# Splitting seven experts' weights where they are used instead of staging them through DRAM, in a fused attention and mixture-of-experts kernel

## The chip, the cores and the metric

The kernel runs on one core of a Trainium2 chip. The metric is the time of one execution on the device, in microseconds; of several runs the median counts. The core has TensorE (matrix products), VectorE, ScalarE and GpSimd (elementwise work on 128 partitions), SyncE (here it only issues DMAs) and 16 DMA engines that all queues share. Each engine runs its own instruction stream in order, and the streams meet only in semaphores.

## What is computed

Four sequences of 512 tokens with 256 features attend to four contexts of 1024 tokens, and each token then goes through a shared expert and two of eight routed experts:

```python
x = x + tanh(g_xattn) * attention(layernorm(x), ctx, ctx, Wq, bq, Wk, bk, Wv, bv, Wo, bo)   # 16 heads of 16
z = layernorm(x)
shared = swiglu(z @ sw1 + sb1) @ sw2 + sb2
probs  = softmax(z @ gate_w + gate_b);  top 2 of 8 experts
routed = sum over the 2 experts of prob * (swiglu(z @ rw1[e] + rb1[e]) @ rw2[e] + rb2[e])
x = x + tanh(g_ffn) * (shared + routed)
```

All data are float32. Each of the nine experts (shared and eight routed) has 2*512 + 2*256 = 1536 weights on each of 128 partitions, 768 KB.

## The kernel before

Nearly every product is made as a sum of parts: a float32 operand is split into a high part (the value in TensorE's reduced float32 format) and a low part (the value minus the high part), and three products of parts are added. So each expert's weights must be cast and subtracted once before use. The result takes 24 units of 128 columns in the tile `wall`, 12 of the high part and 12 of the low part.

Phase A projects queries, keys and values for four batches (`b`). The attention loop follows: 16 units, four batches times four groups of four heads (`u`), and in each unit eight key blocks (`k`). TensorE makes the scores, ScalarE the exponentials, TensorE the sums of values, and beside that TensorE and VectorE find the row maxima for the next unit, which GpSimd splits in three parts (`split_max`).

During attention the local memory has no room for all experts. Two experts (EARLY) are split into their place by GpSimd in the first units (`prepare`). The seven others (LATE) have their places where attention keeps its operands. In the units 2 to 8 GpSimd's `stage(e)` splits one each in a buffer `wraw` and sends both parts to the DRAM tensor `w_parts`; `raw_in` loads the next. In the last batch places come free unit by unit, and SyncE's `late_weights(e, nth)` loads both parts of one expert, 1536 KB, each load after the one before it has landed: the first three during the units 1 to 3 of the last batch, the fourth when all scores are made, the fifth when all values are summed, the last two once batch 3's attention output has been turned.

The last batch is unrolled, with router work beside attention: for batch 0 to 2, TensorE turns the attention output (`r_attn`, L1564), multiplies by Wo (`r_wo`, L1571), VectorE adds it to x and takes the layer norm's statistics (`r_sum`, L1157 first) and scales (`r_scale`, with nine small operations in L1172 to L1174 and four scalings in L1176), TensorE turns and makes the logits, VectorE ranks the experts (`r_choose`) and makes the token slots (`r_slots`). The orders are written out by hand for every engine. `r_attn(b)` on TensorE waits for `wo_taken`, b times, that is for L1157 of the batch before.

After attention comes the hand-off: the same steps for batch 3, with the shared expert's first and second products (`first`, `second`) in between, ScalarE's `silu` and `gated_high`, VectorE's `gate`, `gated_low` and `base`. GpSimd scatters the normalised rows with indirect DMAs into `zs`, ordered by expert (`scatter`). Between `scatter(1)` and `scatter(2)` GpSimd blanks a tile `fill` and writes blank rows to `acc`, and SyncE writes blank rows and their ids to the spare rows of `zs`. Then 39 tiles of 128 routed tokens follow, each with the weights of its expert, whose place and number TensorE reads from a table made at run time; GpSimd adds each tile's result to `acc` with an indirect DMA, and at the end `acc` is copied to the output.

## Time and profile before

| | us |
|---|---|
| median of 3 timed runs | 705.16 |
| lowest and highest | 701.01, 708.19 |
| span of the profiled execution, first to last instruction | 716.3 |
| TensorE busy in it | 643.1 (90%) |
| VectorE busy | 482.2 (67%) |
| ScalarE busy | 424.1 (59%) |
| GpSimd busy | 229.7 (32%) |

The profiled execution's own time beside its span isn't given; its span alone is 11.1 us above the timed median. Phase A takes the first 105 us or so, the attention loop lasts until about 514, the hand-off until 583.7, and the tiles until about 699. A busy share is an average over these stretches; what ends a wait must be read from each.

### The profile page before, as it was taken

How to read it: one execution, taken by the hardware profiler on the slowest of the kernel's cores; microseconds unless marked ns; L12 is line 12 of the kernel's file. 1: busy time of each engine (PE TensorE's matmuls, PEld its weight loads, DVE VectorE, ACT ScalarE, POOL GpSimd, SP SyncE). 2: the span in 40 equal slices, each digit the busy share in tenths (PEclk: the TensorE clock that was granted, in tenths of full speed). 3: DMA queues.
4: the chain of work that ended last, by engine and by line, in shares of the span. 5: the costliest groups of instructions: out<-in, count | busy, mean ns of one | idle time of the engine just before them, and what ended most of it. 6: DMA issues, size and time to landing. Idle time of an engine off the chain costs nothing.

```text
span 716.3 us, 12642 instructions
## 1 busy us (share of the span) xinstructions
PE 643.1 (90%) x3603; PEld 335.5 (47%) x3616; DVE 482.2 (67%) x805; ACT 424.1 (59%) x842; POOL 229.7 (32%) x240
## 2 busy tenths in 40 slices
PE   3997769699999999999999999999885989999990
PEld 3775542123233333333333333355363778888880
DVE  4786878668888888888888888838726843443330
ACT  4675344567777777777777777767513224544440
POOL 2343242213431443134000221020175414555552
PEclk9999997989999999999999999999986999999995
DMA  7999889754688678966664370250386355555545
GB/s 232 343 251 336 200 257 159 124 76 108 147 159 200 197 162 147 218 185 161 97 103 59 62 117 1 89 208 30 137 299 217 135 174 97 98 95 94 78 49 141
DMA packets 82978, 108.21 MB, mean 151 GB/s; under 512 B 16552, under 2 KB 64690, under 8 KB 81973
## 3 DMA queue, kind: packets, MB, share of 16 engines
q1 hardware_dynamic: 72200, 78.97, 47.7%
q0 software_dynamic: 10736, 28.71, 15.0%
q8 instruction: 22, 0.36, 0.2%
q14 instruction: 20, 0.16, 0.1%
HBM read 62.10 MB, written 47.35 MB: 153 GB/s over the span
## 4 chain that ended last, share of the span: by engine, by line
PE 71%; issue 14%; POOL 5%; DVE 3%; DMA 3%; another core or an unknown queue 1%; ACT 1%; POOLq 1%; SPq 0%; DVEq 0%; ACTq 0%
PE psO L1503 17%; PE psS L1476 16%; PE psM L1458 13%; PE psH L1721 7%; PE psY L1747 3%; PE psH L1677 3%; POOL parts L610 3%; PE psX L1571 1%; PE psX L1709 1%; PE psH L1732 1%; DMA acc<-ysb,ids 1%; DMA wA_raw<-wqkv 1%; PE psO L1546 1%; PE psX L1663 1%
## 5 line engine op out<-in xcount | busy, mean ns | idle before, releaser
L1109 DVE TENSOR_REDUCE mneg<-psM 128x1 f32<-128x1024 f32 x240 | 282.8, 1220 | 67.7 <-PE psM L1458 67.6
L843 ACT ACTIVATE pr<-psS 128x512 f32<-128x512 f32 x488 | 266.7, 595 | 102.1 <-PE psS L1476 102.1
L1476 PE MATMUL psS<-kq 99*128 99x512 bf16 x488 | 153.8, 388 | 7.0 <-DMA kq<-msb 6.3
L1503 PE MATMUL psO<-pr,vt 128*32 128x512 f32 x1024 | 137.2, 608 | 0.0
L1458 PE MATMUL psM<-kq 96*128 96x512 bf16 x480 | 128.2, 388 | 4.4 <-DVE mneg L1109 2.7
L1476 PEld LDWEIGHTS psS<-kq 99*128 99x128 bf16 x488 | 39.9, 97 | 155.4 <-ACT pr L843 130.3
L750 POOL DMA_INDIRECT acc<-ysb,ids x39 | 60.2, 1543 | 69.0 <-ACT ysb L966 37.3
L1458 PEld LDWEIGHTS psM<-kq 96*128 96x128 bf16 x480 | 46.7, 98 | 63.6 <-DVE mneg L1109 8.4
L596 POOL TENSOR_TENSOR msb<-mcp,none 16x128 bf16<-16x128 f32 x16 | 6.2, 389 | 209.1 <-ACT mcp L820 209.0
L1721 PE MATMUL psH<-wall,zgT 128*128 x234 | 68.2, 427 | 1.5 <-DVE zgT L1341 1.5
L1347 DVE TENSOR_TENSOR rg<-psH,rs 128x256 f32<-128x256 f32 x39 | 16.6, 425 | 66.3 <-ACT rs L954 64.6
L1721 PEld LDWEIGHTS psH<-wall,zgT 128*128 128x128 f32 x234 | 44.5, 190 | 8.2
L610 POOL TENSOR_TENSOR parts<-kf,parts 128x512 bf16<-128x512 f32 x24 | 30.5, 1285 | 55.0 <-ACT parts L791 55.0
L954 ACT ACTIVATE rs<-psH 128x256 f32<-128x256 f32 x39 | 14.9, 383 | 42.8 <-PE psH L1721 41.7
L705 POOL DMA_INDIRECT zs<-zx,slot_u x32 | 32.2, 1006 | 23.4 <-DVE slot_u L1228 13.5
L1747 PE MATMUL psY<-wall,gT 128*128 x234 | 37.0, 294 | 0.0
L1503 PEld LDWEIGHTS psO<-pr,vt 128*32 128x32 f32 x1024 | 20.2, 108 | 35.5 <-issue 33.8
L1677 PE MATMUL psH<-zT,wall 128*128 128x512 f32 x96 | 29.5, 452 | 5.6 <-issue 5.6
L1747 PEld LDWEIGHTS psY<-wall,gT 128*128 128x128 f32 x234 | 30.2, 189 | 0.5
L966 ACT ACTIVATE ysb<-psY,zg 128x256 f32<-128x256 f32 x39 | 18.6, 476 | 17.4 <-PE psY L1747 14.7
L1416 PE MATMUL psV<-wAH,tH 128*128 128x256 f32 x64 | 16.7, 347 | 12.2 <-DVE tL L1027 12.2
L1033 DVE TENSOR_REDUCE mneg<-psO 128x1 f32<-128x1024 f32 x16 | 19.6, 1223 | 9.3 <-PE psO L1400 9.1
(243 smaller groups left out, 821.1 us busy)
## 6 DMA issues: line engine op xcount, KB each, us to landing
kq<-k_parts SPq DMA_DIRECT2D x96, 128.0 KB, 5.7
w_parts<-wraw POOLq DMA_DIRECT2D x14, 768.0 KB, 4.3
wall<-w_parts SPq DMA_DIRECT2D x7, 1536.0 KB
v_pad<-vst SPq DMA_DIRECT2D x16, 512.0 KB, 8.7
vt<-v_pad SPq DMA_DIRECT2D x16, 512.0 KB, 7.6
wraw<-wexp POOLq DMA_DIRECT2D x9, 768.0 KB, 7.2
k_parts<-parts SPq DMA_DIRECT2D x16, 384.0 KB, 6.3
kq<-q_parts SPq DMA_DIRECT2D x96, 64.0 KB, 5.3
```

What stands on the lines that cost most here:

```text
L610: nc.gpsimd.tensor_tensor(parts[:, c, m, 2], kf[:, m], parts[:, c, m, 1], ALU.subtract).then_inc(k_ok, 1)
L705: nc.gpsimd.indirect_dma_start(out=zs[:, :], out_offset=bass.IndirectOffsetOnAxis(ap=slot_u[:, b, k * QT + t:k * QT + t + 1], axis=0), in_ ...
L750: nc.gpsimd.indirect_dma_start(out=acc[:, :], out_offset=bass.IndirectOffsetOnAxis(ap=ids[:, i:i + 1], axis=0), in_=ysb[:, i % YB], in_off ...
L843: nc.scalar.activation(pr[:, slot, j], score_bank(s, j), ACT.Exp, scale=SCALE).then_inc(e_done, 1)
L1033: V.tensor_reduce(mneg[:, 0, i:i + 1], psE, X_AXIS, ALU.max, negate=True).then_inc(m_free, 1)
L1109: V.tensor_reduce(mneg[:, parity, i:i + 1], psM[:, i % 2], X_AXIS, ALU.max, negate=True).then_inc(m_free, 1)
L1458: last = mm(psM[:, i % 2, half * BLK:(half + 1) * BLK], qst[0:SROWS, slot, h, qt * P:(qt + 1) * P], kst[0:SROWS, slot, h, half * BLK:(half ...
L1476: mm(score_bank(s, j), kst[:, slot, j, kt * P:(kt + 1) * P], qst[:, slot, j], start=True, stop=True).then_inc(s_full, 1)
L1503: last = mm(psO[j * VW:(j + 1) * VW, u % 2], vt[:, u, k, j * VW:(j + 1) * VW], pr[:, k % 4, j], start=(k == 0), stop=(k == KT - 1), skip_g ...
L1677: last = mm(psH[:, j, ab], w1(SH, wp)[:, 4 * k + m], zT(b)[:, zp, k], start=(i == 0 and k == 0), stop=(i == 2 and k == DT - 1))
L1721: last = mm(psR[:, i % 2], zgT[:, i % 2, zp, k], wall[:, bass.ds(w + (12 * wp + 4 * k), 4)].rearrange("p a c -> p (a c)"), start=False, st ...
L1747: last = mm(psQ[:, i % 2, 0:D], gT[:, i % 2, gp, k], wall[:, bass.ds(w + (12 * wp + 8 + 2 * k), 2)].rearrange("p a c -> p (a c)"), start=F ...
```

## The change

- GpSimd no longer stages. `w_parts`, `stage` and `raw_in` go.
- `late_weights(nth)` loads the raw weights of one expert, 768 KB, into the half of its place in `wall` that will hold the low part. The order of the experts (LATE_ORDER) and the points at which the loads are issued stay.
- The cast goes into the other half, and the subtraction then overwrites the raw weights in place. The first three loads are split by GpSimd (`late_split`) after its last bias addition, the other four by a cast on ScalarE (`late_high`) and a subtraction on VectorE (`late_low`), at the places shown in the diff.
- TensorE waits for these splits ahead of the first tile, not for the loads.
- The blank rows are made and written by GpSimd (`blanks`) in unit 2, with all three DMAs on GpSimd's queue.
- GpSimd's table reads of wait counts are now made with a check of their bounds, 16 to 16 times the table's size (`add_waits`).

```diff
-    w_parts = dram("w_parts", [LATE, P, 2 * WCOLS], F32)
+        raw_late = [nc.alloc_sbuf_tensor_at(f"raw_late{e}", [P, WCOLS], F32, offset=W0 + (LU + WU * e + 12) * 4 * UNIT) for e in range(LATE)]
...
+        LATE_ORDER = (LATE - NG, LATE - NG + 1, LATE - NG + 2, LATE - 1, 0, 1, 2)
+        BY_POOL = 3
...
-            def late_weights(e, nth):
-
+            def late_weights(nth):
+
+                e = LATE_ORDER[nth]
                 if nth:
                     sp.wait_ge(wl_ld, 16 * nth)
-                sp.dma_start(wall[:, w_at(e):w_at(e) + WU].rearrange("p u c -> p (u c)").bitcast(F32),
-                             w_parts[e]).then_inc(wl_ld, 16)
+                sp.dma_start(late_raw(e), wexp[raw_of(e)]).then_inc(wl_ld, 16)
...
-            sp.wait_ge(wp_st, 32 * LATE)
...
-            sp.wait_ge(fill_ok, 2)
-            spare_rows = zs[NR * REGION:SLOTS].rearrange("(k p) c -> p k c", p=P)
-            sp.dma_start(spare_rows[:, :, 0:264], fill[:, 0:264].unsqueeze(1).to_broadcast([P, SPARES, 264])).then_inc(fill_st, 16)
-            sp.dma_start(spare_rows[:, :, 264:272], spare_ids).then_inc(fill_st, 16)
...
+            def blanks():
+
+                nc.gpsimd.memset(fill, 0.0).then_inc(fill_c, 1)
...
+                nc.gpsimd.dma_start(acc[NB * NQ:].rearrange("(k p) d -> p k d", p=P),
+                                    fill[:, 0:D].unsqueeze(1).to_broadcast([P, 1 + SPARES, D])).then_inc(added, 16)
+                spare_rows = zs[NR * REGION:SLOTS].rearrange("(k p) c -> p k c", p=P)
+                nc.gpsimd.dma_start(spare_rows[:, :, 0:264], fill[:, 0:264].unsqueeze(1).to_broadcast([P, SPARES, 264])).then_inc(spare_st, 16)
+                nc.gpsimd.dma_start(spare_rows[:, :, 264:272], spare_ids).then_inc(spare_st, 16)
+
+            def late_split(nth):
+
+                e = LATE_ORDER[nth]
+                pool.wait_ge(wl_ld, 16 * (nth + 1))
+                nc.gpsimd.tensor_copy(late_part(e, 0), late_raw(e)).then_inc(lw_phi, 1)
+                pool.wait_ge(lw_phi, nth + 1)
+                nc.gpsimd.tensor_tensor(late_part(e, 1), late_raw(e), late_part(e, 0).bitcast(F32), ALU.subtract).then_inc(lw_pok, 1)
...
-                if 3 <= n < 2 + LATE:
-                    raw_in(n - 2)
                 split_max(n + 1, (n + 1) % 2)
...
-                    if n == 1:
-                        raw_in(0)
-                elif n < 2 + LATE:
-                    stage(n - 2)
+                elif n == EARLY:
+                    blanks()
             bias_x(NB - 1)
+            for nth in range(BY_POOL):
+                late_split(nth)
...
+            def late_high(nth):
+
+                e = LATE_ORDER[nth]
+                act.wait_ge(wl_ld, 16 * (nth + 1))
+                nc.scalar.copy(late_part(e, 0), late_raw(e)).then_inc(lw_hi, 1)
+
             r_exp(2)
             nc.scalar.activation(warm[:], tg_in[:, 1:2], ACT.Silu)
             r_attn(3)

+            late_high(3)
+            late_high(4)
             silu(0, 0)
+            late_high(5)
             gated_high(0, 0)
             silu(0, 1)
             silu(1, 0)
+            late_high(6)
             r_high(3)
...
+            def late_low(nth):
+
+                e = LATE_ORDER[nth]
+                dve.wait_ge(lw_hi, nth - BY_POOL + 1)
+                V.tensor_tensor(late_part(e, 1), late_raw(e), late_part(e, 0).bitcast(F32), ALU.subtract).then_inc(lw_ok, 1)
+
             r_choose(2)
             r_slots(2)
+            late_low(3)
+            late_low(4)
             gate(0, 0)
             gated_low(0, 0)
             r_sum(3)
...
             r_low(3)
+            late_low(5)
             gated_low(0, 1)
...
             r_table_rest()
+            late_low(6)
             base(0)
...
-            pe.wait_ge(wl_ld, 16 * LATE)
+            pe.wait_ge(lw_pok, BY_POOL)
+            pe.wait_ge(lw_ok, LATE - BY_POOL)
```

## Rows read from the trace of the kernel before

**Rows 1.** The page's section 4: the chain that ended last, by engine.

```profile
PE 71%; issue 14%; POOL 5%; DVE 3%; DMA 3%; another core or an unknown queue 1%; ACT 1%; POOLq 1%; SPq 0%; DVEq 0%; ACTq 0%
```

**Rows 2.** Timeline of GpSimd: start, length, engine, line, operation, out<-in, count, idle before.

```profile
208.86 0.39 POOL L596 TENSOR_TENSOR msb<-mcp,none 16x128 bf16<-16x128 f32 x1 [10.06 <-ACT mcp L820]
...
210.66 1.45 POOL L672 CAST wraw<-wraw 128x1536 fp32r<-128x1536 f32 x1
212.19 3.44 POOL L674 TENSOR_TENSOR wraw<-wraw 128x1536 fp32r<-128x1536 f32 x1
...
232.38 0.39 POOL L596 TENSOR_TENSOR msb<-mcp,none 16x128 bf16<-16x128 f32 x1 [9.67 <-ACT mcp L820]
...
373.52 0.39 POOL L596 TENSOR_TENSOR msb<-mcp,none 16x128 bf16<-16x128 f32 x1 [21.67 <-ACT mcp L820]
...
397.04 0.39 POOL L596 TENSOR_TENSOR msb<-mcp,none 16x128 bf16<-16x128 f32 x1 [21.68 <-ACT mcp L820]
```

**Rows 3.** Timeline of GpSimd: its first operation after attention.

```profile
514.32 0.31 POOL L711 MEMSET b_sh<- 128x256 bf16 x1 [42.39 <-PE psO L1503]
```

**Rows 4.** Timeline of SyncE's queue, last batch and hand-off (length: issuing alone).

```profile
477.43 0.34 SPq L493 DMA_DIRECT2D a_in<-attn  x1
478.61 0.61 SPq L457 DMA_DIRECT2D wall<-w_parts  x1
...
515.38 17.00 SPq L457 DMA_DIRECT2D wall<-w_parts  x3
```

**Rows 5.** Timelines of VectorE and TensorE, last batch.

```profile
478.38 0.17 DVE L1172 SCALAR_TENSOR_TENSOR nt<-rstd 128x4 f32<-128x4 f32 x1
...
480.15 1.38 DVE L1176 TENSOR_SCALAR zx<-xs,mv,rstd 128x256 f32<-128x256 f32 x4
482.86 1.28 DVE L1157 SCALAR_TENSOR_TENSOR xs<-psX,tg,xs 128x1024 f32<-128x1024 f32 x1 [1.33 <-PE psX L1571]
...
484.63 1.04 PE L1564 MATMUL psX<-idn,a_in 128*128 128x128 f32 x8
```

**Rows 6.** Timeline of phase A, GpSimd and VectorE.

```profile
29.80 2.42 POOL L610 TENSOR_TENSOR parts<-kf,parts 128x512 bf16<-128x512 f32 x2 [4.34 <-ACT parts L791]
...
30.19 0.92 DVE L1011 TENSOR_TENSOR nt<-rstd 128x4 f32<-128x4 f32 x1
31.14 1.09 DVE L1012 TENSOR_TENSOR nt<-nt,veps 128x4 f32<-128x4 f32 x1
```

**Rows 7.** Timelines of TensorE, VectorE and ScalarE, hand-off.

```profile
524.61 3.70 PE L1571 MATMUL psY<-wo_s,aT 128*128 128x256 f32 x16
...
527.58 0.19 DVE L1223 SCALAR_TENSOR_TENSOR pt<-rank,psX 128x32 f32<-128x32 f32 x1 [5.27 <-remote]
...
529.66 0.69 DVE L1299 TENSOR_TENSOR gL<-g,gH 128x512 fp32r<-128x512 f32 x1 [0.69 <-ACT gH L915]
538.22 1.28 DVE L1157 SCALAR_TENSOR_TENSOR xs<-psY,tg,xs 128x1024 f32<-128x1024 f32 x1 [7.86 <-remote]
...
538.34 1.26 ACT L905 ACTIVATE g<-psH,b_s 128x512 f32<-128x512 f32 x2 [8.71 <-remote]
```

**Rows 8.** Windows: stretch, us, busy (count) by engine, PEclk, DMA share, GB/s.

```profile
478.00:484.00 6.00, 6.00 (x36) 3.51 (x28) 4.29 (x16) 3.51 (x8) 0.00 (x0) 1.00 0.84 294
...
522.00:524.00 2.00, 2.00 (x6) 1.53 (x6) 0.28 (x2) 0.00 (x0) 1.65 (x2) 0.60 0.83 320
```

**Rows 9.** Lines L1058 and L764: ns min/median/max, first and last start.

```profile
L1058 DVE TENSOR_TENSOR wAL<-wA_raw,wAH x2: 686/955/1224, 9.6 to 13.2; 128x1024 fp32r<-128x1024 f32 x1, 128x512 fp32r<-128x512 f32 x1
...
L764 ACT CAST wAH<-wA_raw x2: 613/828/1044, 8.6 to 11.6; 128x1024 fp32r<-128x1024 f32 x1, 128x512 fp32r<-128x512 f32 x1
```

**Rows 10.** Timelines of VectorE and TensorE, end of the hand-off.

```profile
553.01 0.69 DVE L1299 TENSOR_TENSOR zT<-g,zT 128x512 fp32r<-128x512 f32 x1 [3.22 <-ACT zT L915]
...
574.25 1.28 DVE L1304 SCALAR_TENSOR_TENSOR xs<-psX,tg,xs 128x1024 f32<-128x1024 f32 x1 [1.09 <-remote]
...
576.08 0.44 PE L1660 MATMUL psX<-b_sh,uone 128*128 128x256 bf16 x1
```

More of the change, by code:

```diff
@@ L272, in raw_of, with late_raw, late_part @@
             return (e + 1) % NE
+        LATE_ORDER = (LATE - NG, LATE - NG + 1, LATE - NG + 2, LATE - 1, 0, 1, 2)
+        BY_POOL = 3
+        def late_raw(e):
+            return raw_late[e][:]
+        def late_part(e, part):
+            return wall[:, w_at(e) + 12 * part:w_at(e) + 12 * (part + 1)].rearrange("p u c -> p (u c)")
         def w1(e, part):
@@ L297, in table, with add_waits @@
                 tab[0:1, at:at + n], engines=(engine,), min_val=0, max_val=top, skip_runtime_bounds_check_because=SAFE)[1]
+        def add_waits(engine, at, n):
+            return nc.values_load_multi_w_load_instructions(
+                tab[0:1, at:at + n], engines=(engine,), min_val=16, max_val=16 * TAB)[1]
         T_W, T_E, T_ROW, T_WAIT = NR, NR + TAB, NR + 2 * TAB, NR + 3 * TAB
@@ L512, in _ @@
             sp.dma_start(b2_sh[0:3], b2_parts[:, NR * D:NE * D]).then_inc(b2_in, 16)
-            late_weights(0, NG)
+            late_weights(NG)
             sp.wait_ge(o_taken, UNITS + 1)
             sp.wait_ge(at_full, NB)
-            for e in range(1, LATE - NG):
-                late_weights(e, NG + e)
-            sp.wait_ge(fill_ok, 2)
-            spare_rows = zs[NR * REGION:SLOTS].rearrange("(k p) c -> p k c", p=P)
-            sp.dma_start(spare_rows[:, :, 0:264], fill[:, 0:264].unsqueeze(1).to_broadcast([P, SPARES, 264])).then_inc(fill_st, 16)
-            sp.dma_start(spare_rows[:, :, 264:272], spare_ids).then_inc(fill_st, 16)
+            for nth in range(NG + 1, LATE):
+                late_weights(nth)
             def store_base(b):
@@ L543, in _ @@
             sp.wait_ge(sc_last, 16 * 2 * QT)
-            sp.wait_ge(fill_st, 16 * (2 + NR))
+            sp.wait_ge(fill_st, 16 * NR)
+            sp.wait_ge(spare_st, 32)
             sp.wait_ge(tab_ok, 2)
@@ L667, in prepare @@
                 pool.wait_ge(w_ok, nth + 1)
-            def stage(e):
-                pool.wait_ge(raw_ld[0], 16 * (2 + e))
-                nc.gpsimd.tensor_copy(wraw[:, 1].bitcast(F32R), wraw[:, 0]).then_inc(wp_hi, 1)
-                pool.wait_ge(wp_hi, e + 1)
-                nc.gpsimd.tensor_tensor(wraw[:, 0].bitcast(F32R), wraw[:, 0], wraw[:, 1], ALU.subtract).then_inc(wp_ok, 1)
-                pool.wait_ge(wp_ok, e + 1)
-                nc.gpsimd.dma_start(w_parts[e, :, 0:WCOLS], wraw[:, 1]).then_inc(wp_st, 16)
-                nc.gpsimd.dma_start(w_parts[e, :, WCOLS:2 * WCOLS], wraw[:, 0]).then_inc(wp_st, 16)
-            def raw_in(e):
-                pool.wait_ge(wp_st, 32 * e)
-                nc.gpsimd.dma_start(wraw[:, 0], wexp[raw_of(e)]).then_inc(raw_ld[0], 16)
+            def blanks():
+                nc.gpsimd.memset(fill, 0.0).then_inc(fill_c, 1)
+                pool.wait_ge(fill_c, 1)
+                nc.gpsimd.tensor_copy(fill[:, 264:272].bitcast(U32), spare[:, 0:1].to_broadcast([P, 8])).then_inc(fill_ok, 1)
+                nc.gpsimd.tensor_copy(spare_ids.bitcast(U32), spare[:, 1:1 + SPARES].unsqueeze(2).to_broadcast([P, SPARES, 8])).then_inc(fill_ok, 1)
+                pool.wait_ge(fill_ok, 2)
+                nc.gpsimd.dma_start(acc[NB * NQ:].rearrange("(k p) d -> p k d", p=P),
[9 more added lines that the diff above has]
+                nc.gpsimd.tensor_tensor(late_part(e, 1), late_raw(e), late_part(e, 0).bitcast(F32), ALU.subtract).then_inc(lw_pok, 1)
             for n in range(UNITS - 1):
@@ L713, in _ @@
             scatter(1)
-            pool.wait_ge(wp_st, 32 * LATE)
-            nc.gpsimd.memset(fill, 0.0).then_inc(fill_c, 1)
-            pool.wait_ge(fill_c, 1)
-            nc.gpsimd.tensor_copy(fill[:, 264:272].bitcast(U32), spare[:, 0:1].to_broadcast([P, 8])).then_inc(fill_ok, 1)
-            nc.gpsimd.tensor_copy(spare_ids.bitcast(U32), spare[:, 1:1 + SPARES].unsqueeze(2).to_broadcast([P, SPARES, 8])).then_inc(fill_ok, 1)
-            pool.wait_ge(fill_ok, 2)
-            nc.gpsimd.dma_start(acc[NB * NQ:].rearrange("(k p) d -> p k d", p=P),
-                                fill[:, 0:D].unsqueeze(1).to_broadcast([P, 1 + SPARES, D])).then_inc(added, 16)
             nc.gpsimd.iota(row_i[:, 0:16], pattern=[[P, 16]], base=0, channel_multiplier=0).then_inc(io_c, 1)
@@ L740, in _ @@
                 if i % 4 == 0:
-                    waits = table(mybir.EngineType.Pool, T_WAIT + i, 4, 16 * TAB)
+                    waits = add_waits(mybir.EngineType.Pool, T_WAIT + i, 4)
                 pool.wait_ge(ry_ok, i + 1)
```

6 lines of the change are left out of this document (3 added, 3 removed).

## Prediction

> **What bounds the kernel now.** I read the page first: 71% of the chain that ended last lies on TensorE [rows 1]. So an edit counts only where it makes TensorE wait, or lets it start earlier. I then read the timelines of single engines over the three stretches that the diff touches: the attention loop, its last batch, and the hand-off from attention to the expert tiles.
>
> In the attention loop GpSimd repeats one pattern for each unit of four heads: four small operations on the maxima, then, in seven of the units, one late expert's staging. The distance from one unit to the next is 23.52 us (208.86 to 232.38) with staging, and 23.52 us (373.52 to 397.04) without [rows 2]. Staging is free: GpSimd has the time, and nobody waits for the DMAs.
>
> In the last batch the router runs beside attention. VectorE's work is no longer a free-running reduction there but a chain of small operations on which TensorE's next step waits [rows 5], and GpSimd is idle for 42.39 us after its last bias addition, which ends at 471.93 [rows 3].
>
> In the hand-off the output sum of batch 3 (L1157) is the step that everything waits for: batch 3's normalising, turning, logits, slots, scatter and table all follow. In this execution VectorE reached that wait at 530.35 us and left it at 538.22, although TensorE's output projection for it, the 16 matmuls from 524.61, lasts 3.70 us; ScalarE stood still until 538.34, and a shorter wait of VectorE's of the same kind ended at 527.58 [rows 7]. The trace names no releaser for them. Three late loads are in flight from 515.38 on [rows 4], so this wait may belong to the change.
>
> The profiled execution took 716.3 us from first to last instruction, the timed runs a median of 705.16 (701.01 to 708.19), which is at least 11.1 us less. The unexplained waits add up to 7.86 us and some 2.8 us (VectorE went on at 527.58, and the slot matmuls of batch 2, for which it waited, stand ahead of the projection that began at 524.61 [rows 7]): about 10.7. So the timed runs may hold little of them. Their own spread, 7.2 us, is about the size of the longer wait, and the median lies 4.15 us above the lowest; I read that as a median run holding some 4 us of it at most. I make the sum step by step against the profile and say at each step what changes for a timed run.
>
> **Part 1: staging leaves the attention loop.** Seven casts of 1.45 us, seven subtractions of 3.44 us and 21 DMAs leave GpSimd. By the two equal periods above this is worth 0. Bounds: the largest thing it could give is the variation between periods, under 0.1 us a unit; I take 0. The blank rows (a memset, two copies, three DMAs) go into one unit that loses 4.9 us of staging, so they too cost 0; their 2 MB leave the hand-off. GpSimd's short work for them stood ahead of its wait for batch 3's slots, so nothing is won there. Adding a checked table read on GpSimd to every fourth tile lies in waits for TensorE's tiles: 0, at most 0.5 us at the end.
>
> **Part 2: three experts split by GpSimd in the last batch.** Each takes 1.45 + 3.44 us [rows 2], 14.7 us in all, in a hole of 42.4 us. GpSimd's own time is covered. What is not covered is VectorE. Early in the kernel there is a clean picture of the two together: a GpSimd tensor_tensor runs from 29.80 in two pieces to 32.22; VectorE's product of two SBUF tiles of 128x4, 0.17 us in a quiet stretch (L1172 [rows 5]), takes 0.92 us and ends at 31.11, and the next takes 1.09 us and ends at 32.23 [rows 6]. Each waited for one whole GpSimd operation, and one such product gets in between two. No row shows a GpSimd cast beside such a product; the two ends are that it blocks like the subtraction and that it doesn't block. I take that it blocks, as the nearest row is another GpSimd operation that reads SBUF.
>
> The Trainium skill ("SBUF — State Buffer", section "Who interferes with whom") states for this case that a VectorE instruction with two SBUF inputs contends with any GpSimd instruction that reads SBUF, and that whichever starts first holds the shared ports to its end. That speaks against this change. With it the cast blocks too and this part costs what is worked out next; if only the subtraction blocked, it would cost what rival (a) does. No run yet shows which for the cast; for the subtraction the trace agrees (0.92 and 1.09 us).
>
> Now the times. Split 0 runs from 472.0 to about 476.9; VectorE has only one-input work then. The second load had landed before by 478.61, when the next was issued behind it [rows 4], and half as many bytes land some 2 us earlier. So split 1 runs next: cast 477.0 to 478.5, subtraction 478.6 to 482.1. Exactly there stand the nine two-input operations of r_scale(0), from 478.38 to 480.1 [rows 5]. One slips in, the second waits until 482.1. The third load is issued right behind the attention rows' load at 477.43 [rows 4]. The two, 1.3 MB together, take 4.4 us at the 294 GB/s that this stretch moves [rows 8]; with a start near 478.3 and the landing itself that is about 483.2. With eight operations, one each 0.20 us, to go from 482.1, r_scale(0) would need until 483.7, so the cast of split 2 catches its last ones, and the subtraction behind it holds them until about 488.2. Then come the four scalings (1.38 us) and the output sum r_sum(1) (1.28 us), which ends at 491.0 instead of 484.14. TensorE's turn r_attn(2), at 484.63 without a wait [rows 5], waits for exactly that sum. Queued behind it in program order are all remaining scores and values of attention. Cost: 491.1 - 484.6 = 6.5 us. Bounds: 0 (nothing blocks) and 9.8 (both splits in full); I take 6.5.
>
> A pause of that length also costs clock: after the short pauses around the end of attention the granted clock was still 0.60 in 522 to 524 us, between the levels of 1.2 and 2.4 GHz, with TensorE busy throughout [rows 8]. Five busy microseconds at the 1.2 GHz level instead of 2.4 would lose 2.5 us; 0 if the clock holds. I take 1.0, because the stretch is shared with ScalarE's exponentials, which do not slow.
>
> **Part 3: four experts split by ScalarE and VectorE in the hand-off.** VectorE's subtraction of 128x1024 took 1.224 us and of 128x512 0.686 [rows 9]; 512 more columns give 0.538, so 128x1536 takes 1.76 us. ScalarE's casts of the same two shapes took 1.044 and 0.613 [rows 9]: 1.48 for one of 1536. Casts 3 and 4 stand in ScalarE's wait for the first shared-expert matmuls and cost 0. The subtractions 3 and 4 stand on VectorE between the slots of batch 2 and gate(0,0), which leads to ScalarE's cast, gated_low and the sum L1157: 3.5 us on the path. Slots, gate, ScalarE's cast and gated_low together took 2.78 us, from 527.58 to 530.36 [rows 7]. If TensorE's releases are prompt, that work starts at 524.8 and ends at 527.6, so the sum starts with the end of the projection, at 528.35, before the change, and at 524.8 + 2.8 + 3.5 = 531.1 after it: +2.8. In the profiled execution it started at 538.22; if VectorE resumes at 527.58 as there, and the half-size loads, landed by about 530, hold nothing longer, it starts at 527.6 + 2.8 + 3.5 = 533.9: -4.3. For a median run, holding some 4 us of the wait, that is between -1.2 and +2.8. I take the middle, +0.8. Ends: -7.1 (all waits go) and +2.8.
>
> Subtraction 5 lies in VectorE's wait of 3.22 us for ScalarE [rows 10]: 0; if that cover is gone it is 1.76. Subtraction 6 stands ahead of base(0), and through it base(1) is late. base(1) ended at 575.53, TensorE began second(2), which needs it, at 576.08 [rows 10]: 0.55 to spare, and VectorE waited 1.09 us for no named reason before it. So between 0.1 and 1.76; I take 1.0. The tiles need all splits only after second(3).
>
> **Sum.** 0 + 6.5 + 1.0 + 0.8 + 1.0 = +9.3 us. On the median: 714.5 us, +1.3%.
>
> **Rivals.** (a) The lock bites once: the third load lands after 483.7, or a cast doesn't block. Then r_scale(0) ends about 485.1, r_sum(1) 486.4, TensorE waits 1.9 us and the clock holds: 705.2 + 1.9 + 0.8 + 1.0 = 708.9. For it: half a microsecond of landing time decides. (b) It doesn't bite, because VectorE's short operations overtake GpSimd: 707.0. Against it: rows 6. (c) Full hand-off price, no hidden wait in timed runs: 6.5 + 2.5 + 2.8 + 1.76 = 13.6, 718.7. For it: the 11.1 us between profile and median. (d) On the other side, faster: the long wait is caused by the late loads, it exists in timed runs, and half the bytes (2.4 MB instead of 4.7 from 515 on, with 2 MB of blanks gone as well) end it before VectorE arrives: -7.1 + 1.0 = -6.1, 699.1; up to 1.1 more if VectorE's unnamed wait before base(1) goes too, 698.0. It decides the sign only if GpSimd's splits cost under 6 us. For it: VectorE and ScalarE resumed within 0.12 us of each other. Against it: a load of the same size, issued at 478.61, stopped nobody: TensorE was busy in all of 478 to 484 [rows 8].
>
> The Trainium skill ("Runtime: NRT & Kernel Launch", section "Instruction fetch mechanics") has the engines' instructions refilled by DMA, which would give rival (d) a mechanism. No row here shows a fetch that ends at 538.
>
> **Chances.** Forecast 0.43 (own range 710 to 719); (a) 0.18; (b) 0.10; (c) 0.16; (d) 0.13. A measurement of this kernel can tell about 1% (7 us) from no change. Slower by over 1% (above 712.2): (c) and four fifths of the forecast, 0.50. Faster by over 1% (below 698.1): 0.10, the faster half of (d) and what I have not thought of on that side. Within: 0.40. Range 702 to 720: below it (d), above it a tail of (c).
>
> **What would show it.** In the profile after: GpSimd's two groups from about 477 and 483; one L1173 or L1174 operation of over 3 us there; TensorE idle before the turn r_attn(2) for about 6 us; attention units unchanged before that. In the hand-off two subtractions of 1.76 us ahead of gate(0,0), and L1157 of batch 3 less than 6 us after them. The prediction is wrong if TensorE has no pause before that turn (then b), or if L1157 of batch 3 follows the end of attention by some 7 us less than now (then d).

## The result

The changed kernel takes **717.76 us** (median of 4 runs, 716.59 to 719.49) against 705.21 (4 runs, 701.01 to 708.19) for the kernel before: a ratio of **1.020, 95% interval 1.016 to 1.025**, 12.6 us slower. Measured again beside the staging kernel it was 1.018 (1.010 to 1.026). A timed run takes some 1.9 us more than the span from first to last instruction: the execution profiled below has a span of 716.9 us and took 718.75.

The kernels were timed in five series, each with the kernel before beside the others; it took 705.2, 702.0 and 702.4 us in three of them and 716.0 and 715.8 in the two others, and the profile of before shown ahead of the prediction carries most of what makes up that difference (111.18 us from r_sum(0) to the first tile product, against 98.45 in an undisturbed profile). So each ratio below is against before in its own series, and stages are compared among undisturbed profiles. The changed kernel itself was timed only in the quicker series. Ratios and their intervals leave out a run that lies far above the others of its kernel.

**The page of the kernel after.** Section 1 (busy time, share, instructions) and section 4 (the chain by engine):

```profile
PE 639.2 (89%) x3616; PEld 334.3 (47%) x3616; DVE 497.2 (69%) x809; ACT 430.1 (60%) x846; POOL 204.9 (29%) x213
...
PE 68%; issue 15%; DVE 7%; POOL 4%; DMA 3%; ACT 1%; POOLq 1%; SPq 0%; DVEq 0%; ACTq 0%
```

VectorE's share of the chain grew from 3% to 7% [rows 1]: it now holds others up. TensorE's own work is about the same (639.2 us busy, 643.1 before).

**The last batch.** SyncE's queue (issue time, length of issuing alone), then GpSimd's timeline with the three splits:

```profile
477.06 38.55 SPq L473 DMA_DIRECT2D raw_late<-wexp  x2
...
522.84 10.84 SPq L473 DMA_DIRECT2D raw_late<-wexp  x3
```

```profile
471.10 1.45 POOL L696 CAST wall<-raw_late 128x1536 fp32r<-128x1536 f32 x1
472.63 3.46 POOL L698 TENSOR_TENSOR wall<-raw_late,wall 128x1536 fp32r<-128x1536 f32 x1
476.04 1.46 POOL L696 CAST wall<-raw_late 128x1536 fp32r<-128x1536 f32 x1
477.58 3.45 POOL L698 TENSOR_TENSOR wall<-raw_late,wall 128x1536 fp32r<-128x1536 f32 x1
481.84 1.46 POOL L696 CAST wall<-raw_late 128x1536 fp32r<-128x1536 f32 x1 [0.81 <-DMA raw_late<-wexp]
483.39 3.42 POOL L698 TENSOR_TENSOR wall<-raw_late,wall 128x1536 fp32r<-128x1536 f32 x1
```

The third load is issued at 477.06, behind the attention rows, and GpSimd takes it up at 481.84; the last three follow one another from 522.84.

VectorE's timeline of the same time, r_scale(0) and r_sum(1) (L1173):

```profile
475.12 1.41 DVE L1177 BATCH_NORM_STATS2 stats<-xs 128x6 f32<-128x256 f32 x4
...
476.97 0.56 DVE L1184 TENSOR_SCALAR veps<-mv 128x4 f32<-128x4 f32 x1
477.56 0.17 DVE L1185 TENSOR_SCALAR nt<-veps 128x4 int32<-128x4 int32 x1
477.77 3.30 DVE L1186 TENSOR_SCALAR rstd<-nt 128x4 int32<-128x4 int32 x1
...
481.88 1.44 DVE L1189 TENSOR_TENSOR nt<-nt,veps 128x4 f32<-128x4 f32 x1
...
483.56 3.27 DVE L1188 SCALAR_TENSOR_TENSOR nt<-rstd 128x4 f32<-128x4 f32 x1
...
488.55 1.27 DVE L1173 SCALAR_TENSOR_TENSOR xs<-psX,tg,xs 128x1024 f32<-128x1024 f32 x1
```

Put the two side by side by their end times. L1184 ends at 477.53 with the cast (477.50). L1186 ends at 481.07 with the subtraction (481.03), L1189 at 483.32 with the third cast (483.30), L1188 at 486.83 with the last subtraction (486.81). Each takes 0.16 or 0.17 us elsewhere [rows 5]. The statistics (L1177), which ran beside the first subtraction, were not held: 1.41 us, as in any profile.

TensorE meanwhile (the turn r_attn(2) is L1590), and the granted clock (PEclk, third from the end) around it:

```profile
489.93 1.94 PE L1590 MATMUL psX<-idn,a_in 128*128 128x128 f32 x8 [5.94 <-issue]
...
493.50 1.75 PE L1529 MATMUL psO<-pr,vt 128*32 128x512 f32 x8
```

```profile
473.80:488.55 14.75, 10.19 (x60) 5.15 (x58) 14.23 (x25) 8.05 (x15) 12.04 (x5) 0.99 0.28 104
488.55:499.29 10.74, 9.36 (x41) 6.26 (x42) 6.99 (x29) 3.44 (x6) 0.00 (x0) 0.70 0.00 0
```

```profile
484.00:488.00 4.00, 0.00 (x0) 0.00 (x0) 3.89 (x6) 1.09 (x3) 2.81 (x1) 1.00 0.00 0
...
489.00:494.80 5.80, 4.87 (x22) 2.91 (x22) 5.28 (x24) 2.35 (x4) 0.00 (x0) 0.50 0.00 0
```

The turn had no wait before [rows 5]; now TensorE stands 5.94 us, until r_sum(1) is done. The granted clock falls to the 1.2 GHz level (0.50) at about 488.1, while TensorE still stands, and is back at 494.8, so that TensorE's first 4.87 us of work run at that level and the turn takes 1.94 us instead of 1.04. Over r_sum(1) to r_sum(2) that averages 0.70.

**The hand-off.** VectorE (L1327 is the late subtraction, L1173 is r_sum(3), L1320 base(0)), then TensorE (L1597 the projection, L1608 the turn, L1686 second(2)):

```profile
532.26 3.42 DVE L1327 TENSOR_TENSOR wall<-raw_late,wall 128x1536 fp32r<-128x1536 f32 x2
...
537.02 0.69 DVE L1315 TENSOR_TENSOR gL<-g,gH 128x512 fp32r<-128x512 f32 x1 [0.69 <-ACT gH L921]
537.63 1.27 DVE L1173 SCALAR_TENSOR_TENSOR xs<-psY,tg,xs 128x1024 f32<-128x1024 f32 x1
...
548.84 1.75 DVE L1327 TENSOR_TENSOR wall<-raw_late,wall 128x1536 fp32r<-128x1536 f32 x1
...
552.51 0.69 DVE L1315 TENSOR_TENSOR zT<-g,zT 128x512 fp32r<-128x512 f32 x1 [1.32 <-ACT zT L921]
...
568.98 1.74 DVE L1327 TENSOR_TENSOR wall<-raw_late,wall 128x1536 fp32r<-128x1536 f32 x1
570.65 1.27 DVE L1320 SCALAR_TENSOR_TENSOR xs<-psY,tg,xs 128x1024 f32<-128x1024 f32 x1
```

```profile
531.36 3.70 PE L1597 MATMUL psY<-wo_s,aT 128*128 128x256 f32 x16
...
545.01 1.97 PE L1608 MATMUL psX<-idn,zx 128*128 128x128 f32 x8 [4.43 <-DVE zx L1192]
...
575.41 0.27 PE L1686 MATMUL psX<-b_sh,uone 128*128 128x256 bf16 x1 [3.09 <-DVE xs L1320]
```

The projection ends at 535.06 and r_sum(3) starts at 537.63: the two subtractions at 532.26 stand on the path, and no wait without a named releaser is left of those in [rows 7]. Subtraction 5 (548.84) lies in a wait; its remainder is 1.32 us where it was 3.22 [rows 10]. Subtraction 6 (568.98) leads straight into base(0), and TensorE's wait for base(1) grows to 3.09 us from the 1.43 us of an undisturbed profile of staging (before_bounded_2).

### The profile page after: what moved, and what is told of

It is laid out like the page before. It is cut to its first block, busy times and chain, and to the rows that moved or that the text cites. A ratio compares the mean times of both kernels' runs of the same rounds, so it can differ in the third digit from the quotient of the medians.

```text
span 716.9 us, 12714 instructions
## 1 busy us (share of the span) xinstructions
PE 639.2 (89%) x3616; PEld 334.3 (47%) x3616; DVE 497.2 (69%) x809; ACT 430.1 (60%) x846; POOL 204.9 (29%) x213
## 4 chain that ended last, share of the span: by engine, by line
PE 68%; issue 15%; DVE 7%; POOL 4%; DMA 3%; ACT 1%; POOLq 1%; SPq 0%; DVEq 0%; ACTq 0%
PE psO L1529 17%; PE psS L1502 16%; PE psM L1484 13%; PE psH L1747 7%; PE psY L1773 3%; POOL parts L620 3%; PE psX L1597 1%; PE psH L1703 1%; PE psH L1744 1%; PE psX L1735 1%; PE psH L1758 1%; DMA acc<-ysb,ids 1%; PE psO L1572 1%; DVE wall L1327 1%; DMA wA_raw<-wqkv 1%
## 5 line engine op out<-in xcount | busy, mean ns | idle before, releaser
L1484 PE MATMUL psM<-kq 96*128 96x512 bf16 x480 | 126.6, 384 | 5.3 <-DVE mneg L1125 3.5
L719 POOL DMA_INDIRECT zs<-zx,slot_u x32 | 35.7, 1115 | 15.0 <-issue 9.6
L982 ACT ACTIVATE ysb<-psY,zg 128x256 f32<-128x256 f32 x39 | 18.6, 476 | 17.3 <-PE psY L1773 14.7
L1703 PE MATMUL psH<-zT,wall 128*128 128x512 f32 x96 | 25.4, 421 | 0.0
L791 ACT ACTIVATE parts<-psF,bq_s 128x512 bf16<-128x512 f32 x24 | 16.3, 687 | 14.5 <-PE psF L1456 13.0
```

The source lines that it names most:

```text
L719: nc.gpsimd.indirect_dma_start(out=zs[:, :], out_offset=bass.IndirectOffsetOnAxis(ap=slot_u[:, b, k * QT + t:k * QT + t + 1], axis=0), in_ ...
L982: nc.scalar.activation(ysb[:, i % YB], psQ[:, i % 2, 0:D], ACT.Identity, scale=zg[:, i % ZG, bass.ds(e + D, 1)]).then_inc(ry_ok, 1)
L1484: last = mm(psM[:, i % 2, half * BLK:(half + 1) * BLK], qst[0:SROWS, slot, h, qt * P:(qt + 1) * P], kst[0:SROWS, slot, h, half * BLK:(half ...
L1703: last = mm(psH[:, j, ab], w1(SH, wp)[:, 4 * k + m], zT(b)[:, zp, k], start=(i == 0 and k == 0), stop=(i == 2 and k == DT - 1))
```

## Experiments

All kernels below have the four waits of the tile loop loaded with asserted bounds, as the change has them. Times are medians with the ratio to before in the same series. The stages of the undisturbed profiles, each the difference of two start times in the timelines (r_sum(b) and base(0) on VectorE, tile_first on TensorE), in us:

| kernel | r_sum(0) to (1) | (1) to (2) | (2) to (3) | r_sum(3) to base(0) | to tile_first | sum |
|---|---|---|---|---|---|---|
| before_bounded_2 | 8.27 | 8.70 | 36.69 | 30.76 | 14.03 | 98.45 |
| no_splits_spaced | 8.26 | 8.71 | 36.73 | 30.83 | 13.86 | 98.39 |
| after | 14.75 | 10.74 | 38.34 | 33.02 | 14.91 | 111.76 |
| after_again | 14.62 | 10.78 | 38.35 | 33.03 | 14.06 | 110.84 |
| pool_later | 8.27 | 8.70 | 39.19 | 33.42 | 14.34 | 103.92 |
| hand_off_spread | 14.70 | 9.89 | 36.90 | 34.29 | 13.97 | 109.75 |
| both_moved | 8.26 | 8.70 | 37.16 | 32.67 | 13.90 | 100.69 |

What follows tile_first takes 130.3 to 131.4 us in all seven. What lies ahead of r_sum(0) isn't in the table: r_sum(0) starts at 470.97 to 474.12 us in the seven, and at 469.65, 471.73 and 474.60 in three profiles of the staging kernel. All of that spread arises ahead of the third unit of attention. From GpSimd's first operation on that unit's maxima to r_sum(0) it is 312.67 to 312.72 us in after, after_again, pool_later, both_moved and hand_off_spread, and the same in the staging kernel's profiles (312.67 in before_bounded_2, 312.73 in before): taking staging out gives attention nothing.

The last stage of after is 0.85 us longer than that of after_again because the clock fell once more, to 0.50 in 578 to 580 us, behind the same 3.1 us wait for base(1) after which it stayed whole in after_again.

**1. GpSimd's splits 1 and 2 later.**

```
 def late_split(nth):
     e = LATE_ORDER[nth]
+    if nth:
+        pool.wait_ge(zn_ok, nth + 1)
     pool.wait_ge(wl_ld, 16 * (nth + 1))
```

> The changed kernel with GpSimd's splits 1 and 2 held back by a wait on the scaled rows: split 1 starts after r_scale(1), split 2 after r_scale(2). Theory A (the splits hold VectorE's r_scale(0), TensorE's r_attn(2) stands still, and its clock falls): the 5.9 us pause ahead of r_attn(2) and the stretch at the low clock go, 8 to 9 us less: 708 to 711 us. Theory B (the pause is there for another reason, for example the order of the router's steps beside attention, now that nothing is staged): the time stays at 716 to 719 us. Theory C (the splits only move the pause: they hold r_sum(2) or r_shift(0) instead): 1 to 3 us are given back, 710 to 713 us, with a VectorE instruction of 1.5 or 3.4 us at the new place.

Measured: 708.3 us, 1.009 of before (1.006 to 1.013). GpSimd's timeline, the moved splits:

```profile
487.70 1.46 POOL L698 CAST wall<-raw_late 128x1536 fp32r<-128x1536 f32 x1 [12.97 <-DVE zx L1194]
489.25 3.47 POOL L700 TENSOR_TENSOR wall<-raw_late,wall 128x1536 fp32r<-128x1536 f32 x1
497.96 1.47 POOL L698 CAST wall<-raw_late 128x1536 fp32r<-128x1536 f32 x1 [5.25 <-DVE zx L1194]
```

TensorE's turn and the granted clock over r_sum(1) to r_sum(2) (third from the end):

```profile
482.47 1.04 PE L1592 MATMUL psX<-idn,a_in 128*128 128x128 f32 x8
```

```profile
480.70:489.40 8.70, 8.70 (x53) 5.31 (x52) 7.00 (x27) 5.77 (x11) 1.62 (x2) 1.00 0.03 13
```

Theory A holds. The same work on the same engine, 13 and 17 us later counted from r_sum(0), costs attention nothing: the first two stages are the staging kernel's to 0.01 us, TensorE has no wait, the clock is whole. At its new place a split runs beside a product with one operand in PSUM and beside the output sum and statistics, and none of them waits.

**2. The subtractions of the hand-off spread out.** ScalarE's casts 4 and 5 go behind gated_high(0,0), and on VectorE:

```
-late_low(3)            # both ahead of gate(0, 0)
-late_low(4)
...
+late_low(3)
 r_low(3)
-late_low(5)
+late_low(4)
...
 r_choose(3)
+late_low(5)
 r_slots(3)
...
-late_low(6)
 base(0)
...
 base(2)
+late_low(6)
 base(3)
```

> The changed kernel with ScalarE's and VectorE's splits put into gaps of the hand-off: ScalarE's casts 4 and 5 behind gated_high(0,0), VectorE's subtractions 3 and 4 around r_low(3), 5 ahead of r_slots(3), 6 between base(2) and base(3). Theory A (the subtractions 3 and 4 stand ahead of r_sum(3) and cost 2.5 us of path there, and the one ahead of base(0) up to 3 more by second(2)): 712 to 716 us, that is 2 to 5.5 us less than the changed kernel. Theory B (the hand-off is set by TensorE's own work, and the subtractions cost nothing): 717 to 718.5 us. Theory C (a subtraction at a new place holds GpSimd's scatters or TensorE's r_logits(3)): over 719 us.

Measured: 712.0 us, 1.014 (1.010 to 1.017). The 2.5 us ahead of r_sum(3) are back (from the start of the projection's last matmul to r_sum(3) it is 0.41 us, 2.96 in the changed kernel), but r_sum(3) to base(0) grew from 33.0 to 34.3: subtractions at places that looked idle were in part on the path. The hold in attention is there as before (14.70), but behind it the clock fell some two microseconds before r_sum(1) and only 3 us of TensorE's work ran at the lower level, so the next stage takes 9.89 us and not 10.74. Theory A, at the low end of its range.

**3. Both.**

> The changed kernel with both edits: GpSimd's splits 1 and 2 behind r_scale(1) and r_scale(2), and ScalarE's and VectorE's splits spread over the gaps of the hand-off. Theory A (two separate costs that add up, 8.5 and 3.5 us): 703 to 708 us, within 1% of the kernel before, since staging itself was hidden and its removal is worth nothing. Theory B (removing the staging is worth something that the two costs covered up): under 701 us. Theory C (the costs overlap, so that one edit takes what the other would): 709 to 712 us.

Measured: 708.88 us, 1.009 (1.005 to 1.013). The profile does what theory A says: 100.69 us in the table, 10.2 to 11.1 less than the changed kernel and 2.2 more than the staging kernel. The timed runs say otherwise: 708.88 lies just above theory A's range, between it and C's, and the runs (705.4 to 711.6) are no faster than pool_later's. Of the 6.9 us over before the stages explain 2.2. Another 2.4 us of the profile lie ahead of the third unit (161.45 us against 159.06 in before_bounded_2), where the staging kernel's own profiles differ by 4.9. And the length of a low-clock stretch changes between executions: with the same hand-off order hand_off_spread took 34.29 us from r_sum(3) to base(0) and this kernel 32.67, with a granted clock of 0.57 and 0.79 in eight microseconds of TensorE's work there:

```profile
547.50:555.50 8.00, 7.70 (x24) 6.33 (x25) 6.61 (x17) 4.24 (x6) 5.50 (x6) 0.57 0.31 114
```

```profile
543.50:551.50 8.00, 7.96 (x32) 6.59 (x32) 6.14 (x17) 4.00 (x5) 3.95 (x4) 0.79 0.25 90
```

The first row is hand_off_spread, the second both_moved. Whether these two make up the rest in the timed runs isn't shown.

**4. The bounds alone, and a second profile of staging.** The kernel before, the four waits loaded with `min_val=16`.

> The kernel before with one thing of the change alone: the four waits of the tile loop on GpSimd are loaded with their bounds asserted. A second profile of the staging kernel comes with it. On the bounds: if they cost time in the tile loop, the ratio to before is over 1.003; if not, it is 1.000 within its interval. On the pause of 7.9 us ahead of r_sum(3) in the first profile of before: theory A (it belongs to that execution) has a span of 699 to 705 us, r_sum(3) within 1 us of the end of the projection, and no remote releaser in the hand-off; theory B (it belongs to the kernel, by the late loads of both parts) has the pause again and a span of 712 us or more.

Measured: 714.67 us against 716.0 for before, ratio 0.999 (0.996 to 1.002): the bounds cost nothing. The pause was there again. VectorE's timeline and TensorE's:

```profile
524.74 0.69 DVE L1304 TENSOR_TENSOR gL<-g,gH 128x512 fp32r<-128x512 f32 x1 [0.69 <-ACT gH L920]
533.29 1.28 DVE L1162 SCALAR_TENSOR_TENSOR xs<-psY,tg,xs 128x1024 f32<-128x1024 f32 x1 [7.86 <-remote]
```

```profile
519.67 3.70 PE L1576 MATMUL psY<-wo_s,aT 128*128 128x256 f32 x16
```

The same 7.86 us as in [rows 7]. Theory A of that expectation (it belonged to one execution) fell. The timed runs of this series hold the pause too; those of the series of the result, with before at 705.2, hold none of it, to judge by experiment 5 (703.3 us without it), where I had given a median run some 4 us.

**5. The same kernel in another series, beside the changed one.**

> The staging kernel with bounded waits once more, in one call with the changed kernel. Two profiles of it have the same pause in the hand-off (TensorE's signal for r_sum(3) comes 9.9 us after the projection's last matmul is recorded), while the chips differ: before took 705 and 702 us on two chips and 716 on a third. Theory A (the pause is the difference between the chips): where before is timed at 700 to 706 us, this profile has no pause, r_sum(3) within 1 us of the projection and a span of 700 to 704 us; where it is timed at 714 or more, the pause is there. Theory B (the pause comes with every profile of a kernel that loads both parts): the pause is there whatever the time.

Measured: 703.34 us, 1.0005 (0.996 to 1.005), before at 702.38. Now VectorE shows:

```profile
523.98 0.69 DVE L1304 TENSOR_TENSOR gL<-g,gH 128x512 fp32r<-128x512 f32 x1 [0.68 <-ACT gH L920]
525.39 1.28 DVE L1162 SCALAR_TENSOR_TENSOR xs<-psY,tg,xs 128x1024 f32<-128x1024 f32 x1 [0.72 <-PE psY L1576]
```

No pause, and the projection named as releaser. The kernel is the same, so theory B falls. Theory A falls in its word "chips": the chip on which before took 702.0 took 715.8 in a later series. The pause comes and goes between series, on one chip.

> The changed kernel again, on the chip of the other two. Theory A (its cost is its own: 8.6 us in attention and 2.5 to 4 us in the hand-off): 1.016 to 1.022 of before on any chip. Theory B (on a chip where the staging kernel has the pause in the hand-off, halving the late loads spares the changed kernel some of it): 0.998 to 1.006 of before there, and 1.018 to 1.022 where before is timed at 700 to 706 us.

Measured: 716.11 us, 1.018 (1.010 to 1.026). Theory A, as far as it goes: what the changed kernel takes where the staging kernel has the pause wasn't measured. Against before_bounded_2's stages it loses 6.35, 2.08, 1.66, 2.27 and 0.03 us, 12.4 in all; the timed medians differ by 13.7 (716.11 less 702.38).

**6. All splits left out.** First with seven plain copies of the weights made in one burst beside one unit; in one kernel all splits are out, in one GpSimd's alone (below), in one those of the other two engines:

```
-for nth in range(BY_POOL):
-    late_split(nth)
...
-pe.wait_ge(lw_pok, BY_POOL)
```

> The changed kernel with all seven late splits left out, so that the late experts' two parts are both plain copies of the weights (they are copied once beside attention, and read from there; that part of the computation is changed). What is left of the change is the staging taken out of attention, the blank rows filled there, and the bounded waits. Theory A (the whole loss is in the splits: the hold at r_scale(0) and the instructions in the hand-off): 0.998 to 1.003 of before. Theory B (taking the staging out of attention, or filling the blank rows there, costs something itself, which would account for the 0.9% that is left after both moves): 1.006 to 1.010 of before. Theory C (the removal gains, and the splits ate it): under 0.995.

> The changed kernel with GpSimd's three splits left out (the parts of those three experts are plain copies of the weights), ScalarE's and VectorE's kept where they are. Theory A (the hold of r_scale(0) with the low clock behind it is the larger cost): 1.006 to 1.010 of before, the remainder being the hand-off, and TensorE's r_attn(2) without its pause. Theory B (the pause there has another cause): 1.018 to 1.022, as the changed kernel.

> The changed kernel with the four splits of ScalarE and VectorE left out (the parts of those four experts are plain copies of the weights), GpSimd's three kept where they are. Theory A (the hand-off's splits cost 3.5 us of the 12.6): 1.012 to 1.016 of before. Theory B (they cost nothing, all is GpSimd's): 1.019 or more. If their places cost as much as spreading them over the gaps gave back, the time is that of the spread kernel, 1.014.

Measured: 1.020 (1.014 to 1.026), 1.013 (1.007 to 1.019) and 1.030 (1.024 to 1.036), before at 716.0. Their times tell nothing of the splits: r_sum(0) started at 478.38, 480.04 and 481.84 us where before_bounded, in the same series, had it at 469.65, and r_sum(3) came 14 to 15 us after the start of the projection's last matmul. My copies had disturbed what they were to measure. One reading is free of both: r_sum(0) to r_sum(1) took 8.27 us with all splits gone, 8.26 with GpSimd's gone, and 10.37 with only the hand-off's gone. The hold is GpSimd's. The 10.37 is a single catch: there the third load landed only at 491.95, after the chain, so VectorE was held once (one operation of 3.29 us), TensorE waited 1.56 us, and its turn ran at full clock (1.06 us). One catch costs 2.1 us and two cost 6.35.

Then with one copy beside each of seven units:

```
+elif n <= EARLY + LATE:
+    nc.gpsimd.dma_start(w_plain[n - EARLY - 1],
+        wexp[raw_of(LATE_ORDER[n - EARLY - 1])]).then_inc(parked, 16)
```

> As no_splits (all seven late splits left out, the late experts' parts are plain copies), but the seven copies are made one beside each unit instead of all at once, so that they don't hold attention's own loads (no_splits reached r_sum(0) 4 us later than any other kernel). Theory A (staging and blank rows cost nothing, the whole loss is in the splits): 0.996 to 1.003 of before. Theory B (something else of the change costs about the 0.9% that both_moved kept): 1.006 to 1.010. Theory C (loading both parts of the late experts in the hand-off is what stretches it, whatever is staged): as before or slower where before has the pause, and none where it has none.

Measured: 702.71 us, **0.9985** (0.995 to 1.002), and every stage within 0.2 us of the staging kernel's. Taking staging's casts and subtractions out of attention and filling the blank rows there is worth nothing and costs nothing; the loss is in the seven splits. This kernel still loads two full parts for each late expert, so what the halved loads are worth it doesn't show; after_again, which has them, loses 12.4 us in the stages all the same.

**7. Casts alone.** GpSimd's subtraction replaced by two casts:

```
 nc.gpsimd.tensor_copy(late_part(e, 0), late_raw(e))
-nc.gpsimd.tensor_tensor(late_part(e, 1), late_raw(e), late_part(e, 0), SUBTRACT)
+nc.gpsimd.tensor_copy(late_part(e, 1), late_raw(e))
+nc.gpsimd.tensor_copy(late_part(e, 1), late_part(e, 0))
```

> The changed kernel with GpSimd's subtraction replaced by two further casts in each of its three splits (the low parts of those three experts are copies of the high ones), 4.4 us of casts in place of a cast and a subtraction of 4.9. Theory A (a cast, which reads one tile, shuts VectorE out as the subtraction does): VectorE's instructions in r_scale(0) wait in steps of up to 1.45 us, from r_sum(0) to r_sum(1) takes 12.5 us or more against 8.3 without splits, and the time is 1.014 to 1.019 of before. Theory B (only the subtraction does, the 1.44 us instruction in the changed kernel's r_scale(0) was a coincidence): from r_sum(0) to r_sum(1) 8.3 to 9 us and 1.005 to 1.009 of before.

Measured: 723.2 us (725.4 with one run of 735.19), 1.011 (1.007 to 1.015), before at 715.84. GpSimd's timeline, then VectorE's:

```profile
475.42 1.47 POOL L697 CAST wall<-raw_late 128x1536 fp32r<-128x1536 f32 x1
476.95 1.49 POOL L699 CAST wall<-wall 128x1536 fp32r<-128x1536 f32 x1
482.11 1.47 POOL L696 CAST wall<-raw_late 128x1536 fp32r<-128x1536 f32 x1 [3.67 <-DMA raw_late<-wexp]
```

```profile
475.55 1.36 DVE L1185 TENSOR_SCALAR veps<-mv 128x4 f32<-128x4 f32 x1
476.94 0.17 DVE L1186 TENSOR_SCALAR nt<-veps 128x4 int32<-128x4 int32 x1
477.15 1.32 DVE L1187 TENSOR_SCALAR rstd<-nt 128x4 int32<-128x4 int32 x1
478.50 0.16 DVE L1189 SCALAR_TENSOR_TENSOR nt<-rstd 128x4 f32<-128x4 f32 x1
```

A cast shuts VectorE out to its end as the subtraction does: L1185 ends at 476.91 with the cast (476.89), L1187 at 478.47 with the next (478.44). So theory A on the mechanism. On the size neither holds: 9.19 us from r_sum(0) to r_sum(1) lies between A's 12.5 and B's 9, and 1.011 between their ranges. The chain came free at 478.47, and its last product began at 480.07, two microseconds before the third load landed. In the changed kernel the subtraction kept it until 481.07, so that the third split, starting at 481.84, caught it again. The second catch costs more than the first: part of the first falls into VectorE's wait ahead of r_sum(1) (1.32 us in before_bounded_2).

**8. Other gaps.** Splits 1 and 2 later; subtraction 3 ahead of r_slots(2), 4 behind gated_low(0,1), 5 behind gated_low(3,1), 6 ahead of base(3).

> The changed kernel with GpSimd's splits 1 and 2 held back as in pool_later, and VectorE's four subtractions in other gaps than in both_moved, read from the staging kernel's profile on an undisturbed chip (before_bounded_2): 3 ahead of r_slots(2) (2.4 us idle there), 4 behind gated_low(0,1) (3.1 us idle), 5 behind gated_low(3,1) (1.5 us) and 6 between base(2) and base(3) (2.1 us). Theory A (from r_choose(3) to base(0) VectorE itself is the path, so that both_moved's subtractions ahead of r_low(3) and r_slots(3) still cost 1.9 us): from r_sum(0) to the first tile_first 98.5 to 99.5 us as the staging kernel's 98.45, timed 0.998 to 1.004 of before. Theory B (both_moved's loss is in the low clock behind the hand-off or elsewhere, not in the places): 1.006 to 1.012, as both_moved's 1.009.

Measured: 721.31 us, 1.008 (1.005 to 1.012), before at 715.84. The pause is in this profile:

```profile
534.42 1.28 DVE L1175 SCALAR_TENSOR_TENSOR xs<-psY,tg,xs 128x1024 f32<-128x1024 f32 x1 [7.27 <-remote]
```

So the places can't be judged from it, and A and B of that expectation stay open. One place shows a cost even so: the first tile turn waits 0.79 us for subtraction 6, ahead of base(3). No kernel of this study beats the kernel before; the ratios of pool_later, both_moved and gaps are within 1% of it.

## Why the prediction was near, and which step was off

The sum said +9.3 us; 12.6 was measured, inside the range of 702 to 720 but 3.3 us above the forecast. 12.4 us stand in the stages of after_again, 13.3 in those of the first profile. Step by step, in the prediction's order:

- **Part 1, 0.** Right, by no_splits_spaced (0.9985) and before_bounded (0.999).
- **Part 2, the hold, 6.5.** Right in size and mechanism: 6.35 us from r_sum(0) to r_sum(1), undone by pool_later. The two catches came much as worked out, the third split beginning at 481.84 while the chain still ran. It was close: five products of 0.2 us were left, so one microsecond later there would have been a single catch, 2.1 us in place of 6.35. That the size came out so well is partly luck. Two details were off. VectorE's operations with one SBUF input were held too (L1184 and L1186, both tensor_scalar), where I had only products of two counted; so the catch began earlier, but a held operation costs the rest of GpSimd's, whichever it is. And that a cast blocks, which I had taken from the nearest row, is now shown. The Trainium skill ("SBUF — State Buffer", section "Who interferes with whom") lists copy, cast and tensor_scalar among VectorE's operations that can take both port pairs, where their operands allow it, and so contend with GpSimd: if L1186's do, it is held by that rule, and it was (3.30 us). I had used only its sentence on two inputs.
- **Part 2, the clock, 1.0.** TensorE had 4.87 busy us at the 1.2 GHz level, the five for which the upper bound of 2.5 us was worked out. They cost 2.08 us from r_sum(1) to r_sum(2) and some 0.9 back before r_sum(3): from there r_sum(3) came 1.66 later with 2.54 us of subtraction wait in it (2.96 less 0.42, projection to r_sum(3)). Net 1.2, and 1.4 in hand_off_spread (1.19 and 0.21). The price of the low stretch was near the upper bound; that part of it comes back I hadn't foreseen, and that the clock is the whole reason for these 2.08 us is argued from the two rows, not tested by an edit. A net cost close to the 1.0 that I took is luck: I had guessed between two bounds.
- **Part 3, subtractions 3 and 4, 0.8: the term that was mis-sized most.** They cost 2.5 us. The full price of 2.8 was worked out; I then took the middle of -1.2 and 2.8, because the one profile of before had a pause there of which I gave a median run 4 us, and let the change end it. The pause belongs to neither kernel: before_bounded_2 has none, gaps has it with raw loads. In series without it there is nothing to win back.
- **Subtraction 5, 0.** Right: it lies within the wait.
- **Subtraction 6, 1.0.** r_sum(3) to base(0) grew by 2.27 us: 1.67 of them the subtraction (568.98 to 570.65), where I had taken 1.0 of at most 1.76. The remaining 0.6 lies ahead of it, where the turn runs at the lower clock (1.97 us against 1.09 in before_bounded_2). The path by which I let it cost, base(1) and TensorE's second(2), is real (TensorE waits 3.09 us for base(1)), but it is only one of two. In after_again, pool_later and before_bounded_2 what ends last ahead of the tiles is GpSimd's chain, which I had left out: its last scatters, two memsets, SyncE's loads, and the first tile's rows, for which TensorE waits 0.89, 1.19 and 0.86 us. Subtraction 6 holds that chain by about as much, as the last section shows.

With the full hand-off price the sum is 6.5 + 1.0 + 2.8 + 1.7 = 12.0. Rival (c), full price and no hidden wait in timed runs, was the right case, and its 13.6 is 1 us too high mainly because it took the clock at 2.5. Rival (a) fell (the third split began at 481.84, when five of the chain's products were still to run), though no_hand_off_splits shows its case, with TensorE's wait at 1.56 us where it said 1.9 and the clock whole; (b) fell (TensorE's 5.94 us); and (d) fell twice over: raw loads don't end the pause, and undisturbed runs have none.

## What to carry to other kernels

Work that an idle engine takes on is free only if nothing that it shares is wanted at that time: GpSimd's 14.7 us fitted into a hole of 42 us and still cost TensorE 6 us, through VectorE operations of 0.17 us; a wait on an event of the other engine's chain gave all of that back. A hold that pushes a chain into the next long operation costs more than twice (2.1 us for one catch, 6.35 for two), so see where its end falls and not only its start. Two paths can end within a microsecond of each other, as base(1) and the first tile's rows do here; an edit that frees one of them wins no more than that. When one profile's span is over 1% off the timed median, take a step's full price from its instructions and treat the profile's unnamed waits as belonging to neither kernel until a second profile has them.

## What the runs showed of the hardware

**A pause in the hand-off that comes and goes.** In seven profiles (before, before_bounded, no_splits, no_pool_splits, no_hand_off_splits, gaps, pool_three_casts) r_sum(3) starts 10.3 to 15.3 us after the last matmul of its projection has begun; in the seven others it is 0.41 us, or 2.96 where two subtractions stand ahead of it. TensorE's rows don't show one cause. In gaps the 24 matmuls behind the projection run in 5.86 us, as in before_bounded_2. In before_bounded the projection begins at 519.67, 20 of them run from 523.02 to 528.02, and the last four come with gaps of 0.80 to 1.00 us, the last at 531.77; VectorE gets the projection's signal at 533.29. In before, VectorE and ScalarE went on within 0.12 us of each other [rows 7]. I don't know what holds the signal. It isn't the size of the late loads (both kinds of kernel have it) and not the chip alone (one had both). It falls into the stretch where late loads and scatters run together; more than that the traces don't show.

**VectorE holds GpSimd in turn.** A scatter on GpSimd takes 0.98 us (the first row below, from the changed kernel) and 2.02 when a late subtraction of VectorE (548.84 to 550.58) has begun before it:

```profile
548.13 0.98 POOL L719 DMA_INDIRECT zs<-zx,slot_u  x1 [0.31 <-issue]
549.42 2.02 POOL L719 DMA_INDIRECT zs<-zx,slot_u  x1 [0.30 <-issue]
```

The hold at 549.42 costs nothing, as GpSimd waits 5.12 us for the next slots after this group of scatters. The holds of the last two scatters do cost. In after_again they run into subtraction 6 (567.55 to 569.29) and into the two operations L1315 behind base(0) (570.42 to 571.69); below are these two, then the same two in before_bounded_2:

```profile
568.05 2.11 POOL L719 DMA_INDIRECT zs<-zx,slot_u  x1 [0.30 <-DVE tab L1291]
570.46 2.09 POOL L719 DMA_INDIRECT zs<-zx,slot_u  x1 [0.30 <-issue]
```

```profile
556.65 0.98 POOL L710 DMA_INDIRECT zs<-zx,slot_u  x1 [0.30 <-DVE tab L1280]
557.94 1.53 POOL L710 DMA_INDIRECT zs<-zx,slot_u  x1 [0.30 <-issue]
```

That is 1.7 us more. In after_again the memsets behind the scatters end at 575.58, SyncE's loads behind them start at 575.61, and TensorE waits 0.89 us for the first tile's rows. In the first profile of the changed kernel the same hold is covered, because TensorE was later there by the clock. These 1.7 us don't come on top of what subtraction 6 costs ahead of base(0); they are a second path beside it. That is read from the chain that ended last in each profile, not tested by an edit of its own.
